# Second attention: probabilities split into f16 halves on two engines and turned by DMA, row sums from a ones column of the values

## The reference, cut to what matters

```python
q = query @ Wq + bq                      # 16 heads of 32 columns
k, v = (context @ Wkv + bkv)             # 77 keys
scores = einsum('bhid,bhjd->bhij', q, k) * scale
attn = softmax(scores, axis=-1)          # over the 77 keys
out = einsum('bhij,bhjd->bhid', attn, v)
x = x + tanh(g_xattn[1]) * (out @ Wout + bout)
```

## Time and profile before

| | |
|---|---|
| median of 3 runs | 1884.7 us (1880.64 to 1885.06) |
| profiled execution, its own time | 1882.1 us |
| its span, first to last instruction | 1880.3 us |
| PE busy | 1352.5 us (72%) |
| DVE busy | 1524.7 us (81%) |
| ACT busy | 692.7 us (37%) |
| POOL busy | 250.2 us (13%) |
| transposes issued by SP, of 128x1024 two-byte elements | 16, 3.1 us to landing |

### The profile page before, as it was taken

How to read it: one execution, slowest core, us unless ns; L and a number is a source line. 1 busy time by engine, 2 the same in 40 slices (tenths; PEclk the granted TensorE clock), 3 DMA queues, 4 the chain that set the end, 5 groups by cost and what they waited for, 6 DMA issues and landing times.

```text
span 1880.3 us, 24271 instructions
## 1 busy us (share of the span) xinstructions
PE 1352.5 (72%) x8046; PEld 699.4 (37%) x8120; DVE 1524.7 (81%) x2477; ACT 692.7 (37%) x2105; POOL 250.2 (13%) x197
## 2 busy tenths in 40 slices
PE   4142637779687977698778968797869876987663
PEld 3020214434263435343443435343634353434321
DVE  6989997877887797868787878779787879686796
ACT  2122205542274326342454236432734164415210
POOL 1003300031002200130013100310013001300000
PEclk8556767989899998899899989999999999999887
DMA  9263770033202410043003220142023300420011
GB/s 352 86 207 108 160 174 5 1 50 74 69 2 34 90 48 23 9 82 79 25 7 62 57 69 2 34 90 56 14 34 57 79 24 6 84 57 23 7 27 47
DMA packets 268334, 118.03 MB, mean 63 GB/s; under 512 B 235770, under 2 KB 252666, under 8 KB 265622
## 3 DMA queue, kind: packets, MB, share of 16 engines
q1 hardware_dynamic: 268182, 116.17, 25.4%
HBM read 49.04 MB, written 8.39 MB: 31 GB/s over the span
## 4 chain that ended last, share of the span: by engine, by line
issue 41%; DVE 31%; PE 18%; DMA 3%; ACT 3%; SPq 2%; POOL 2%; POOLq 0%; DVEq 0%; ACTq 0%
PE bank L1094 13%; PE bank L1183 4%; DVE pair L838 4%; DVE amax L829 4%; DVE hid L834 2%; DVE th L882 2%; DMA region<-region 1%; DVE pair L846 1%; SPq L308 1%; ACT region L527 1%; DVE pair L848 1%; DMA hqt<-pair 1%; DVE xb L834 1%; DVE pair L853 1%; DVE stats L678 1%
## 5 line engine op out<-in xcount | busy, mean ns | idle before, releaser
L1183 PE MATMUL bank<-w_dn,region 128*128 128x512 fp8e4 x1024 | 243.4, 386 | 60.7 <-DMA region<-region 60.7
L1094 PE MATMUL bank<-w_up,xt 128*128 128x512 fp8e4 x1024 | 243.3, 384 | 35.0 <-ACT region L491 19.7
L1094 PE MATMUL bank<-w_gate,xqt 128*128 128x512 bf16 x461 | 143.1, 426 | 157.7 <-DVE th L882 107.9
L500 ACT ACTIVATE th<-bank,half_cg 128x512 f32<-128x512 f32 x128 | 88.0, 688 | 383.4 <-PE bank L1094 383.4
L418 POOL TENSOR_TENSOR region<-g,region 128x512 f16<-128x512 f32 x128 | 186.4, 1462 | 317.8 <-ACT region L491 310.4
L882 DVE SCALAR_TENSOR_TENSOR th<-th,bank 128x512 f32<-128x512 f32 x128 | 87.5, 684 | 132.8 <-ACT th L500 132.8
L527 ACT ACTIVATE region<-bank,nm 128x77 f32<-128x77 f32 x512 | 160.7, 349 | 60.1 <-DVE nm L928 60.1
L1094 PE MATMUL bank<-w_down,hqt 128*128 128x512 bf16 x491 | 126.8, 414 | 70.1 <-DMA hqt<-pair 69.4
L1183 PEld LDWEIGHTS bank<-w_dn,region 128*128 128x128 f16 x1024 | 100.9, 99 | 187.9 <-issue 72.5
L488 ACT ACTIVATE g<-bank 128x512 f32<-128x512 f32 x128 | 76.5, 597 | 253.2 <-PE bank L1094 188.2
L1094 PEld LDWEIGHTS bank<-w_up,xt 128*128 128x128 f16 x1024 | 100.8, 99 | 163.2 <-issue 53.1
(11 more groups left out here) (207 smaller groups left out, 2543.7 us busy)
## 6 DMA issues: line engine op xcount, KB each, us to landing
xin<-in_x SPq DMA_DIRECT2D x16, 512.0 KB, 3.9
out_x<-x SPq DMA_DIRECT2D x16, 512.0 KB, 2.8
region<-in_w_up_t SPq DMA_DIRECT2D x1, 4096.0 KB, 12.8
hid<-in_gate_w SPq DMA_DIRECT2D x4, 1024.0 KB, 4.6
x<-in_gate_w SPq DMA_DIRECT2D x4, 1024.0 KB, 4.8
hid<-in_up_w SPq DMA_DIRECT2D x4, 1024.0 KB, 4.6
x<-in_up_w SPq DMA_DIRECT2D x4, 1024.0 KB, 5.0
hid<-in_down_w SPq DMA_DIRECT2D x4, 1024.0 KB, 5.8
```

Source lines behind the costliest of these rows:

```text
L500: eng.activation(th[:, u % 2, :], bank[4][:, :], ACT.Tanh, scale=half_cg[:, :]).then_inc(sg["th"], 1)
L1094: last = mm(out, lhs, rhs, start=(n == 0), stop=(n == len(pairs) - 1))
L1183: last = mm(bank[2 + t % 2][:, :], ht[i][:, t % 2, f, :], w_dn[:, f, :], start=(f == 0 and i == 0), stop=(f == KF - 1 and i == 1))
```

## The change: what it does

- ACT no longer sums rows while it takes exponentials (no `accum_out`, no accumulator read). `rs3` is gone.
- The f32 probabilities are split before they are turned, in their own layout: ACT copies `p3` to f16 (high, step `m + 1`), DVE subtracts (low, step `m + 2`), both from SBUF and on 4x77 columns, into `ps3` (three buffers).
- PE's transposes of `p3` and the ACT and DVE reads of banks 6 and 7 are gone. SP turns both halves of the four heads with one DMA transpose of 128x1024 (`turn_p`), into `pt3` (four buffers, two of which lie in `th`).
- The values carry a 33rd column, ones in the high half and zeros in the low. Each head's product gives 33 columns, the last of which is the row sum. A tile's result lies in two banks (2 and 6, eight heads each), and DVE scales it with two reciprocals and two multiplications.
- The product with the values is 5 steps behind the scores instead of 4 (`PV_LAG`), and all that follows in a tile is one step later too.
- An exponential of step `n` now waits for `p3l` of the four heads two before (its buffer `p3` is read by the subtraction), where it waited for PE's transposes.

```diff
-                if 2 <= n <= TILES * NC + 1:
-                    m = n - 2
-                    want(act, "p3t", g, m + 1)
-                    if m >= 2:
-                        want(act, "o3", g, m - 1)
-                    eng.activation(pt3[0][0:M, m % 2], bank[6 + m % 2][0:M, :].rearrange("p (h t) -> p h t", h=HC),
-                                   ACT.Copy).then_inc(sg["p3h"], 1)
                 if n < TILES * NC:
                     want(act, "nm3", g, n + 1)
                     if n >= 2:
-                        want(act, "p3t", g, n - 1)
+                        want(act, "p3l", g, n - 1)
                     for j in range(HC):
                         last = eng.activation(p3[:, n % 2, j, :], bank[4 + n % 2][:, j * M:(j + 1) * M], ACT.Exp,
-                                              bias=nm3[:, n % 2, j:j + 1], accum_out=rs3[:, t % 2, h:h + 1])
+                                              bias=nm3[:, n % 2, j:j + 1])
                     last.then_inc(sg["p3"], 1)
+                if 1 <= n <= TILES * NC:
+                    m = n - 1
+                    want(act, "p3", g, m + 1)
+                    if m >= 3:
+                        want_pt(act, g, m - 3)
+                    eng.activation(ps3[m % 3][:, 0, :, 0:M], p3[:, m % 2], ACT.Copy).then_inc(sg["p3h"], 1)
...
+            def turn_p(g, m):
+                want(sp, "p3l", g, m + 1)
+                sp.sem_inc(sm["sp_passed"])
+                if m >= 4:
+                    want(sp, "o3", g, m - 3)
+                    sp.sem_inc(sm["sp_passed"])
+                sp.dma_start_transpose(pt3[m % 4].rearrange("p i h t -> p (i h) t"),
+                                       ps3[m % 3].rearrange("p i h t -> p (i h t)")).then_inc(sg[f"pt{m % 4}"], 16)
...
-                if 3 <= n <= TILES * NC + 2:
-                    m = n - 3
+                if 2 <= n <= TILES * NC + 1:
+                    m = n - 2
                     want(dve, "p3h", g, m + 1)
-                    eng.tensor_tensor(pt3[1][0:M, m % 2], bank[6 + m % 2][0:M, :].rearrange("p (h t) -> p h t", h=HC),
-                                      pt3[0][0:M, m % 2], ALU.subtract).then_inc(sg["p3l"], 1)
+                    eng.tensor_tensor(ps3[m % 3][:, 1, :, 0:M], p3[:, m % 2], ps3[m % 3][:, 0, :, 0:M],
+                                      ALU.subtract).then_inc(sg["p3l"], 1)
...
+                    for a in range(2):
+                        hs = slice(a * HEADS // 2, (a + 1) * HEADS // 2)
+                        done(eng.reciprocal(rr3[:, hs].unsqueeze(2), with_sums(a)[:, :, HD:HD + 1]))
+                    settle()
...
-                if 4 <= n <= TILES * NC + 3:
-                    m = n - 4
+                if PV_LAG <= n < TILES * NC + PV_LAG:
+                    m = n - PV_LAG
...
-                    want(pe, "p3l", g, m + 1)
+                    want_pt(pe, g, m)
...
-                        last = product(bank[2][:, es], [(pt3[0][0:M, m % 2, j, :], vals1[0][:, b, es]),
-                                                        (pt3[0][0:M, m % 2, j, :], vals1[1][:, b, es]),
-                                                        (pt3[1][0:M, m % 2, j, :], vals1[0][:, b, es])])
+                        hi, lo = (pt3[m % 4][0:M, i, j, :] for i in range(2))
+                        last = product(with_sums(h // 8)[:, h % 8, :], [(hi, vals1[0][:, b, h, :]), (hi, vals1[1][:, b, h, :]),
+                                                                       (lo, vals1[0][:, b, h, :])])
```

75 lines of the change are left out of this document (34 added, 41 removed).

## The result

The changed kernel takes 1912.2 us (median of 4 executions, 1911.8 to 1914.3) against 1884.9 before (4, 1880.6 to 1886.9): ratio 1.016, 95% interval 1.014 to 1.018. It is 1.6% slower. The forecast was 1868 us, in a range that ended at 1893.

What follows compares the result with a forecast made beforehand. DVE was taken to bound phase A's tail, ACT to be as near the bound in its body, and ACT to set the lone phase's step. Profiled 1882.1 - 14.7 (seven loop phases) - 0.5 (lone phase) + 0.8 (prologue) = 1867.7 us; range 1846 to 1893.

Steps and rivals of the forecast that it cites:

- ring: Phase A: exponentials 0.84, ACT's copy 0.46, DVE's subtraction 0.47 and two hand-overs wait on each other, 1.85 us a turn.
- Body: Part of each loop phase A where the 16 groups of exponentials run (37.1 us): gain 2.8 us.
- Step 13: Loop phase A, numbered by exponentials: its scores stand behind PE's output product, so it takes 3.9 us.
- Step 11: Loop phase A, numbered by exponentials: ACT has 0.9 us of work beside the ring, so it takes 2.2 us.
- Tail: Last 26.0 us of each loop phase A, bounded by DVE: loss 0.7 us.
- on an engine that is not the bound: nothing: PE's four transposes, 0.47 us of its time, go; their removal was costed at no gain or loss.
- The product five steps back finds its data as PE gets to it: DMA transposes in phase A cost nothing up to a landing of about 4.3 us; 3.03 us assumed.
- Lone phase: The single phase A at the end, without `stage1`: about 2 us from earlier `xq`, against ring +2.1; counted as -0.5 us.
- Tail or phase B takes it back: Rival: the 2 us gained a phase are lost again because DVE there waits on others; 1882 us, 7%.
- Ring dearer than its parts: Rival: an exponential costs 0.30 us and not 0.21, the ring 2.21 a turn; 1894 us, 25%.
- Transposes land late: Rival: DMA transposes land at 5.0 us, making 2.05 us a step; 1882 us, 6%.
- The removal pays in full: Rival: the ring does not bind and steps run at ACT's 1.3 us; 1831 us, half of that 1849, 17%.

Runs made afterwards that it cites:

- c_noacc: Kernel before the change, only without the accumulator output of the exponentials (probabilities not normalised): 1874.3 us, ratio 0.993.
- j_lag4_pe15: Changed kernel with the product with the values four steps behind, tile ends one step earlier, and group 15 alone turned by PE: 1890.5 us, ratio 1.002.
- d_lag4: Changed kernel with the product with the values four steps behind instead of five and tile ends one step earlier: 1898.7 us, ratio 1.006.
- a_fill: Changed kernel with four never-read PE transposes of the identity at each of steps 2 to 17: 1911.5 us, ratio 1.013.
- o_pe15: Changed kernel, all lags kept, with only group 15 turned by PE in place of DMA: 1928.1 us, ratio 1.023.
- l_delay: Changed kernel with DVE's maxima of step 1 worked out four times instead of once in each phase A: 1932.3 us, ratio 1.024.
- q: j_lag4_pe15 with four never-read PE transposes at steps 13 to 16 of loop phases and 2 to 19 of the lone phase: 1886.5 us, ratio 1.001.

## Why the prediction was wrong

- **Instructions: right.** Exponentials 0.21 us apart (0.21 forecast), copy 0.48 (0.46), subtraction 0.48 (0.47), ring 1.93 (1.85), landing 3.1 in the median. By the figures of the Trainium skill, ScalarE: Activation LUTs, in the section What ACT_TABLE_LOAD costs, the exponential would take an estimated 0.25; the trace shows the smaller figure.
- **Body: right in mechanism, 2 us short.** 0.9 us were gained, not 2.8. The ring cost 0.08 a step more. Step 13 took 4.96 us and not 3.9: DVE waited for a `stage1` product of PE's behind the output product, and the scaling that I had laid under that wait followed it. Step 11 took 3.0 and not 2.2, with PE at a granted clock of 0.52 (1150.4 to 1153.3) after 2.29 us of waiting for DVE's scaling (26.5 us of such waits in the profile, 8.3 before), a wait that the prediction did not have. With the lag of four the body came out at 33.2 in its steady passes, so the sum was good for that order.
- **Tail: the step that failed.** "Loss 0.7 us" was 4.6 on average and 4.9 in the pass shown. The term that was put at nothing is PE's: of its transposes the prediction says "on an engine that is not the bound: nothing", and it keeps every output product at 2.75 us. PE isn't the bound by work, but DVE waits for three of its products in every tail, and they took 4.45, 3.27 and 3.51 us. That is 3.0 us a tail, and 0.7 and 3.0 make 3.7 of the 4.6 to 4.9; the rest, about 1 us, is put down to waits that come with tile ends a step later and that the forecast had too small. Twice the runs show such an excess passed on in full: 1.4 us in c_noacc, 3.4 between two passes of j_lag4_pe15. Traffic of the DMA engines beside it isn't it: they were busy for 0.82 of the product of 2.75 us at 953.49 (j_lag4_pe15) and for nothing of the one of 4.44 at 1768.88 (d_lag4). What lowers the clock there isn't shown: it fell too where none of PE's work was taken out (c_noacc), and the transposes given back brought it up in the tail (a_fill: 2.76, 2.75, 3.52, tail 2.5 us shorter) and cost as much elsewhere.
- **The transposes' landing: covered less than was said, but not this loss.** "The product five steps back finds its data as PE gets to it" does not hold past step 15, where a step has little in it: PE waits 2.48 us in the pass shown, which the prediction named as a sign of being wrong. In the changed kernel the output product behind it waited longer for DVE, and turning group 15 by PE made that kernel slower (o_pe15). With the lag of four the wait stands on the path of the lone phase (3.35 us).
- **Lone phase.** -0.5 was +7.7. The ring gave 1.2 of it up to the last exponentials (28.3 to 29.5 us between the first and the last group's start), less than the forecast 2.1; the other 6.5 are the same tail, 4.1 of them output products of 5.30, 4.45 and 4.27 us (2.75, 2.76 and 4.43 before). The end behind it gave 3.1 back, where 2 us were forecast for the earlier `xq`.
- **Sum.** 7 x 2.1 gained became 29.4 lost, a miss of 44; the lone phase 8 more; phase B and the end 7 less. That is the 44.5 us between 1867.7 and 1912.2.
- **The rivals.** *Tail or phase B takes it back* named the place, and its price (nothing more than the 2 us) was far too small. *Ring dearer than its parts* named 1894, the time nearest to the result, for a reason that did not hold: by its own reckoning 0.08 a turn costs 68 x 0.08 = 5 us. That number is near by luck. *Transposes land late* did not happen: 3.1 us in the median, as assumed. *The removal pays in full* is ruled out by c_noacc, 13 us for the removed reads.
- **Slips in its sums.** Four exponentials at 0.16 are 0.20 us less and not 0.22, and the middle of the full-pay case is 1849 and not 1846; neither changes anything.

What is shown: the loss in the tail is DVE's waiting, mostly for output products that run at half clock for a part of their time, and a slow one costs its full excess; the ring costs 6 us alone; product and tile ends one step earlier give 13.5 us together; ACT's relief is worth 0.5 us in a loop pass. What isn't shown: what lowers the clock at those products, since no fill kept it up without costing as much, and what the landing alone costs, since the 8 us that group 15 on PE gives with the lag of four come with faster products as well. The parts don't add up either: group 15 on PE gains with one lag and loses with the other.

## What to carry to other kernels

A latency that a pipeline's lag covers in the steady part can be bare at its end: work out the last groups of each phase apart, with the steps as short as they are there, and read whether the wait that shows is the one that ends last. When work leaves an engine that others wait for, read how long its remaining products take by the granted clock before costing the removal at nothing. And before building on a removal, time it alone: leaving out the accumulators showed that some 13 us were to be had from ACT's relief, and in the steady loop almost none.

## What was not expected of the hardware

- Where passes repeat, the loop's period often had one of a few values: 201.3 to 201.5 us (before, c_noacc, d_lag4, j), 204.8 (changed, four passes running), 207.9 to 208.2 (l_delay), 197.9 to 198.0 (before, j and q, single passes). Others stand among them, as 203.1 twice in the kernel before. Against its passes of 201.3, 1.65 us taken from the body gave nothing (c_noacc); 1.5 us put into the changed kernel cost 3.3. What fixes these values wasn't settled.
- Executions of one kernel on one chip differ with its clock: twelve of j_lag4_pe15 go from 1880.5 us at a mean granted clock of 0.875 to 1898.1 at 0.864, in nearly that order (correlation -0.95); seventeen of the kernel before from 1880.8 at 0.896 to 1893.4 at 0.885.
- PE's never-read transposes (a_fill) raised the mean granted clock from 0.858 to 0.880 in the profiled executions and left the time where it was.
- Issuing one transpose of 128x1024 two-byte elements costs SP 1.23 us, and 128 of them between two SBUF buffers landed in 3.0 to 4.9 us:

```profile
DMA to landing us min/median/max: 3.0/3.1/4.9
```
